# One fused block on one core: the routing of 64 tiles in groups of 6, 6 and 4 pairs in place of four groups of 4

## The reference, cut to what matters

```
h = layernorm(x) * (1 + ca) + sa
x = x + ga * attention(h)          # linear attention: sigma(q) sigma(k)^T, causal, plus a retrieval from a memory
h = layernorm(x) * (1 + cb) + sb
x = x + gb * ffn(h)
```

```
gate = softmax(h @ w_gate.T)                          # 8 logits per token
topk_scores, topk_idx = top_k(gate, 2)
hid = gelu(h @ W1[e] + b1[e])                         # 128 -> 512, exact gelu
y   = hid @ W2[e] + b2[e]                             # 512 -> 128
out = sum over the 2 chosen experts of score * y
```

## Time and profile before

| what | value |
|---|---|
| median of 3 runs | 492.51 us (491.37 to 492.91) |
| the profiled execution | 490.82 us, its span 489.0 us |
| DVE busy | 417.5 us, 85% of the span |
| PE busy | 342.1 us, 70% |
| ACT busy | 306.5 us, 63% |
| POOL busy | 304.6 us, 62% |
| DMA | 59.62 MB, mean 122 GB/s |

### The profile page before, as it was taken

The page is one execution under the profiler, slowest core; times in us unless marked ns, Lnnn a source line. Parts: engine busy times, 40 slices in busy tenths (PEclk is TensorE's granted clock), DMA queues, the critical chain, the costliest instruction groups (busy, mean ns, idle before and its releaser), DMA issues.

```text
span 489.0 us, 13386 instructions
## 1 busy us (share of the span) xinstructions
PE 342.1 (70%) x3736; PEld 303.2 (62%) x3737; DVE 417.5 (85%) x1078; ACT 306.5 (63%) x691; POOL 304.6 (62%) x360
## 2 busy tenths in 40 slices
PE   1673664738765785673389999999999999995000
PEld 1462564627664665562269989999999999984000
DVE  1879999889998889885759888989899898988997
ACT  1262483739993998373166676776767677669930
POOL 2208830037774776576777834888888888887760
PEclk9976766958985888587599999999999999999555
DMA  8895000002420333235165564666655665653653
GB/s 211 216 312 207 3 1 0 7 22 99 145 102 33 135 104 109 69 97 167 53 173 149 146 117 111 143 145 141 148 137 141 145 145 137 143 122 95 180 157 107
DMA packets 98774, 59.62 MB, mean 122 GB/s; under 512 B 45872, under 2 KB 92080, under 8 KB 98480
## 3 DMA queue, kind: packets, MB, share of 16 engines
q1 hardware_dynamic: 90544, 42.38, 31.3%
q0 software_dynamic: 8192, 16.79, 13.3%
HBM read 21.75 MB, written 23.10 MB: 92 GB/s over the span
## 4 chain that ended last, share of the span: by engine, by line
PE 47%; DVE 34%; issue 9%; ACT 7%; DVEq 1%; ACTq 1%; POOL 0%; POOLq 0%
PE psA L1296 20%; PE psA L1284 10%; PE psV L1284 5%; PE psH L1284 5%; DVE ATT L812 3%; DVE stats L751 2%; PE psH L1182 2%; DVE X L1107 2%; DVE X L888 2%; DVE w_parts L1021 2%; DVE stats L895 1%; ACT ATT L649 1%; DVE ROW L1104 1%; PE psA L1191 1%; PE psA L1193 1%
## 5 line engine op out<-in xcount | busy, mean ns | idle before, releaser
L536 POOL DMA_INDIRECT expert_rows<-ROW,POS x128 | 130.6, 1020 | 71.4 <-issue 37.2
L1296 PE MATMUL psA<-WST,ATT 128*128 x1704 | 114.0, 220 | 1.7 <-DVE ATT L1077 1.7
L1296 PEld LDWEIGHTS psA<-WST,ATT 128*128 128x128 f16 x1704 | 103.2, 98 | 8.9 <-issue 2.8
L1077 DVE SCALAR_TENSOR_TENSOR ATT<-ATT,f_scales 128x1024 f16<-128x1024 f32 x71 | 91.2, 1284 | 2.5
L551 POOL DMA_INDIRECT ROW<-expert_out,POS x64 | 69.3, 1083 | 29.9 <-issue 26.6
L694 ACT ACTIVATE ATT<-psA,b1T,f_scales 128x256 f32<-128x256 f32 x144 | 69.6, 563 | 27.4 <-PE psA L1284 27.0
L551 POOL DMA_INDIRECT BIG<-expert_out,POS x64 | 67.6, 1056 | 17.7 <-issue 15.9
L1075 DVE TENSOR_SCALAR ATT<-ATT,f_scales 128x1024 f16<-128x1024 f32 x71 | 53.8, 757 | 7.2 <-ACT ATT L694 2.1
L1284 PE MATMUL psA<-WT,WST 128*128 128x256 f16 x432 | 54.4, 277 | 3.1 <-ACT ATT L694 1.6
L694 ACT ACTIVATE ATT<-psV,b1T,f_scales 128x256 f32<-128x256 f32 x70 | 35.7, 561 | 30.7 <-PE psH L1284 30.7
L1182 PE MATMUL psH<-ident,ATT 128*128 128x128 f32 x64 | 14.7, 371 | 47.9 <-DVE ATT L812 47.9
(11 more groups left out here) (246 smaller groups left out, 757.1 us busy)
## 6 DMA issues: line engine op xcount, KB each, us to landing
expert_out<-VP SPq DMA_DIRECT2D x71, 128.0 KB
X<-in_x SPq DMA_DIRECT2D x8, 512.0 KB, 7.0
WST<-in_W SPq DMA_DIRECT2D x2, 2048.0 KB, 14.6
WST<-WT SPq DMA_DIRECT2D x16, 256.0 KB
out<-X SPq DMA_DIRECT2D x15, 256.0 KB, 2.3
expert_rows<-ROW,POS POOLq DMA_INDIRECT x128
GA<-gate_rows SPq DMA_DIRECT2D x1, 2048.0 KB, 10.1
GA<-gate_rows SPq DMA_DIRECT2D x1, 1792.0 KB, 10.9
```

The source lines that it names most:

```text
L536: nc.gpsimd.indirect_dma_start(xg, bass.IndirectOffsetOnAxis(ap=POS[:, k * TILES + t:k * TILES + t + 1], axis=0), ROW[:, t * 2 * D:(t + 1) ...
L1077: nc.vector.scalar_tensor_tensor(out=GL[:, k % 2, :], in0=G[:, k % 2, :], scalar=f_scales[:, 3:4], in1=GH[:, k % 2, :], op0=ALU.mult, op1= ...
L1296: last = mm(psD[k % 2][:, h * D:(h + 1) * D], a[:, k % 2, i:i + TOK], W2S[:, ds(e * 2 * FF + b * FF + m * D, D)], start=(m == 0 and c == 0 ...
```

## The change

The groups are 6, 6 and 4 pairs, so there are three routes and three scatters, of 24, 24 and 16 tiles (48, 48 and 32 indirect DMAs). The phases of the FFN end at slots 17, 41 and 71. The steps 6 to 13 are now three hardware loops: steps 6 and 7, then `route(0)`; steps 8 and 9; steps 10 to 13 (two turns), then `route(1)`. `route(2)` stands where `route(3)` stood. The weight chunks are split in the same steps as before. Two tiles of the set-up move or grow: the buffer for the index lists is 256 columns in place of 512, and the mask `notfirst` has an own tile; the routing scratch (`RT`) grows from 12 x 128 to 12 x 192 columns, since it has 8 columns per tile of the largest group.

```diff
-    GPAIRS = (4, 4, 4, 4)
+    GPAIRS = (6, 6, 4)
...
-        iotaf = passing(512)
+        iotaf = passing(max(GRID, GTM * E))
...
-        notfirst = passing(E * TILES)
+        notfirst = sb("notfirst", [128, E * TILES], f32)
...
-            route(0)
-
-            for g, (first, end) in enumerate(((3, 5), (5, 7))):
+            for w, g, first, end in ((0, 0, 3, 4), (0, 1, 4, 5), (1, 1, 5, 7)):
                 with eng.Fori(first, end) as n:
                     for k in range(2):
-                        step(2 * n + k, k, n, g + 1, **({"weights": (g, 2 * n - 6 + k)} if weights else {}))
-                route(g + 1)
+                        step(2 * n + k, k, n, g, **({"weights": (w, 2 * n - 6 + k)} if weights else {}))
+                if 2 * end - 2 == PAIRS_TO[g]:
+                    route(g)
```

## The result

The kernel after takes 497.62 us (median of 4 runs, 496.51 to 498.67) where the kernel before took 491.94 beside it (4 runs, 491.24 to 492.91): a ratio of 1.0113, with a 95% interval of 1.0091 to 1.0134. That is slower by 5.7 us; 7.4 were forecast. The profiled execution took 496.7 us with a span of 494.6, against 489.0 before: +5.6. Lines of the kernel after have numbers one lower than before (L535 is the scatter, L550 the gather, L567 the register load).

A forecast was written before the change was run, and what follows sets the result against it. DVE paces steps, routes and end, PE the FFN, with POOL a second chain nearly as long. POOL's 14.8 us less its slack of 7.43 gives +7.4 on 492.5: 499.9 us, range 495 to 504.

The forecast's parts named there:

- The chain that sets the end: At the last mix: POOL's last gather 14.8 us later, less its old slack, ends the span 7.4 us later.
- a slack of 7.43: Kernel before: POOL's chain by itself would end the span at 481.57 against 489.0, 7.43 us of slack.
- The scatters: POOL's list: 80 scatters, not 64, behind the second POS; the last ends 15.9 us later, at 302.45.
- The gap ahead of the gathers: POOL between last scatter and first gather: landing wait and register loads unchanged, 12.88 us; first gather at 315.3.
- The routes: DVE's path: one 9.00 us route goes, two grow by 1.45 us each, -6.10 us in all.
- The loops: Steps 6 to 13, three loops in place of two: taken as 0, with ends of -1.4 and +1.4 us.
- DVE's early arrival: At the last mixes: DVE there at 478.5 in place of 484.63, its 6.1 us turning into waiting for POOL.
- DVE and PE set the end: Rival, at the end: POOL's delay is hidden and the end comes 6.1 us earlier, 486.4; chance 0.04.
- Gathers that catch up: Rival, POOL from 315 us on: faster gathers end 6.5 to 11 us sooner, time 489 to 493.5; chance 0.07.
- Scatters held up by DVE's splits: Rival, beside the FFN: 16 moved scatters each held by a 0.757 us split, 12.1 us more, 512; chance 0.03.
- A DVE path that doesn't shorten: Rival, routes and loops: -9.00 + 9.0 + 1.4, POOL's second group 7.5 us later than forecast, 507; chance 0.04.

The follow-up runs named there:

- the doubled loads: Kernel before with its 16 register loads done twice; 493.1 us, ratio 1.0011.
- the pair with two loads: Two register loads of eight in place of 16 of one: kernel after 491.74 us (ratio 0.9982), kernel before 492.73 us (1.001).
- 6, 5, 5: Kernel after with groups of 6, 5 and 5 pairs and steps 6 to 17 written out; 493.77 us, ratio 1.0033.
- 4, 8, 4: Kernel after with groups of 4, 8 and 4 pairs; 518.86 us, ratio 1.0532.
- the kernel before with three loops: Kernel before, groups of 4 kept, steps 6 and 7 and steps 8 and 9 as two loops of one turn each; 490.73 us, ratio 0.997.

## Why the prediction was right, step by step

**The chain that sets the end: right.** The forecast was POOL's 14.8 us less a slack of 7.43; measured, the last gather is 13.2 us later and the span 5.6 longer. The slack is shown by the doubled loads (7.39, to some half a microsecond), POOL as the bound by the pair with two loads.

**The scatters: right.** First at 126.80 (forecast 126.0), 49th at 193.13 (193.36), with a wait of 3.79 (some 4), so the late start cost nothing. The 80 from there took 302.16 - 193.13 = 109.03 us, 1.363 each (forecast 109.1 in all). One reading was too clean: besides its waits for `POS` and the gap, POOL's list before also stood for 2.44 us at 224.82, for the landing of a scatter, and for 2.1 us in all between the gathers beside the FFN, for stored slots. Both lie inside the paces that the sum uses, so the sum didn't suffer.

**The gap ahead of the gathers: the term that was off.** I carried the 12.88 us over unchanged; it was 11.66, which is 1.2 of the 1.8 us by which the span was forecast too long. The gap is not a constant: 11.46 and 12.67 in the kernels with 6, 5, 5 and 4, 8, 4, 13.37 in the kernel before with three loops. The loads themselves took about the same (8.7 us between the first and the last start, 9.0 before). The rest: last scatter -0.3, gathers -0.1 (174.47 against 174.55), landing -0.15 (2.00 after the last gather's end), the end -0.05.

**The routes: a little dearer.** 10.61 and 10.77 us against 9.0: +1.63 and +1.77, where 1.45 was forecast. The price of most instructions was right (0.36 us at 192 columns, 0.355 forecast), but not of all: the sum of `psV` and `BIG` (the kernel before, then after) takes 0.25 us more and not 0.065.

```profile
150.03 0.36 DVE L953 TENSOR_TENSOR BIG<-psV,BIG 128x128 f32<-128x128 f32 x1
...
190.84 0.61 DVE L952 TENSOR_TENSOR BIG<-psV,BIG 128x192 f32<-128x192 f32 x1
```

**The loops: taken as nothing, and the reason was another.** The prediction asked whether the first turn of a loop is slow by the loop's start or by the route ahead of it. The runs show no cost of a loop's start, and a third thing that the prediction didn't have: a loop of two turns makes DVE wait for its own results in each step of either turn, 2.4 us before and 1.3 after, so the change gains some 1.1 us there. Steps 6 to 13 took 74.15 us in this execution and not 76.48, beyond the bound of -1.4; the other 1.2 us are mostly DVE's waits for PE, 1.5 us before and 0.4 here, which differ from one execution to the next. On DVE's path other small terms took it back: this execution was 1.6 us later than the one before already at step 6. That too is mostly the execution: the first `POS` stands at 126.29 here, and between 125.13 and 126.10 in the other kernels with six pairs in the first group. So the FFN began at 238.30 (forecast 237.8). The second `POS` came out right to 0.2 us by errors that cancelled. DVE's early arrival was turned into waits, as forecast (over 10 us; 10.8).

**The rivals.** *DVE and PE set the end*: refuted. The Trainium skill's rule (Perfetto Trace Analysis, section Identifying the Most-Contended Engine: relieve the engine with the highest occupancy first) would have taken the change for a gain; the engine at 85% was relieved, and the time rose because of one at 62%. The runs agree with it once POOL is out of the way: there a route less gave 6.4 us. *Gathers that catch up*: no; they kept their pace to 0.1 us. *Scatters held up by DVE's splits*: no; 1.363 us each over the 80, and 1.39 over the 43 that run from 242.7 us on, where 1.38 was allowed. *A DVE path that doesn't shorten*: no; -5.5 us at the FFN's last slot.

## What to carry to other kernels

When work is merged into fewer, larger batches, look for the in-order list that waits for the batches, and count what stands behind the last wait: here 16 indirect DMAs more behind it cost 22 us of POOL's list and outweighed a stage that went. An engine whose timeline is all but unbroken to near the end, as POOL's was here at 62%, can be the next bound; its slack is the distance from its last instruction's landing to the use, and adding known work to it measures that distance. Once the slack is known, cut the list first (several numbers in one load, no wait that a later one covers), and then the change on the other path pays.

## What the runs showed that I had not expected

A wait ahead of register loads cost more than its own length, since POOL's sequencer otherwise works ahead: without it the gap fell from 5.25 to 0.30 us, where the landing accounted for 2.3. Sixteen loads of one register are some 9 us of POOL's list; two loads of eight took 0.57 to 1.20 us each. And a hardware loop of two turns cost DVE some 0.3 us a step in waits for its own results, which neither a loop of one turn nor the written-out steps show to that extent.
